# 16-head attentions: in odd steps a group of value matmuls stands in front of the scores instead of behind them

## The reference

```
def _L1_xattn_ref(q, k, v, Wq, bq, Wk, bk, Wv, bv, Wo, bo):
    B, L, D, H = (4, 512, 256, 16)
    ...
    qh = _split_heads(q @ Wq.T + bq)
    kh = _split_heads(k @ Wk.T + bk)
    vh = _split_heads(v @ Wv.T + bv)
    scores = jnp.einsum('bhqd,bhkd->bhqk', qh, kh) * SCALE
    attn = jax.nn.softmax(scores, axis=-1)
    out = jnp.einsum('bhqk,bhkd->bhqd', attn, vh)
    out = out.transpose(0, 2, 1, 3).reshape(q.shape[0], q.shape[1], D)
    return out @ Wo.T + bo
...
x = x + _L1_xattn_ref(_layernorm(x, axis=-1), ctx_1024, ctx_1024, ...)
...
x = x + _L3_xattn_ref(_layernorm(x, axis=-1), ctx_1024, ctx_1024, ...)
```

## Time and profile before

| what | value |
|---|---|
| median of 3 runs | 1415.19 us (1411.68 to 1415.5) |
| profiled execution | 1412.58 us, span 1410.6 us |
| TensorE busy | 1255.1 us, 89% of the span |
| VectorE, ScalarE, GpSimd busy | 60%, 33%, 33% |
| mean granted clock of TensorE | 0.962 of full speed |
| first attention, steps 0 to 63 | from 337.00 to 546.99 us of the span |
| second attention, steps 0 to 63 | from 976.98 to 1185.37 us |

### The profile page before, as it was taken

The page is one execution under the profiler, slowest core; times in us unless marked ns, Lnnn a source line. Parts: engine busy times, 40 slices in busy tenths (PEclk is TensorE's granted clock), DMA queues, the critical chain, the costliest instruction groups (busy, mean ns, idle before and its releaser), DMA issues. The chain is left out here.

```text
span 1410.6 us, 31497 instructions
## 1 busy us (share of the span) xinstructions
PE 1255.1 (89%) x9884; PEld 1003.2 (71%) x9884; DVE 851.2 (60%) x2809; ACT 472.5 (33%) x1119; POOL 472.2 (33%) x452
## 2 busy tenths in 40 slices
PE   4999789997899998799898899898899998799995
PEld 3777589995566665598787666776566665599994
DVE  6788444445677776344575477664566776366663
ACT  3556111112556554011111244443555554011110
POOL 1244612223224434422322256532134343222231
PEclk9999899998999999899999999999999999899998
DMA  9001334322101301564554100000001111645523
GB/s 309 36 24 40 113 112 137 126 65 75 46 24 39 133 33 54 198 196 140 169 180 144 47 14 1 1 1 23 8 24 40 33 44 46 226 94 138 138 48 86
DMA packets 86180, 120.07 MB, mean 85 GB/s; under 512 B 11248, under 2 KB 63600, under 8 KB 85776
## 3 DMA queue, kind: packets, MB, share of 16 engines
q1 hardware_dynamic: 45984, 51.53, 12.0%
q10 hardware_dynamic: 25856, 35.14, 7.8%
q0 software_dynamic: 14224, 31.92, 7.8%
HBM read 82.53 MB, written 38.13 MB: 86 GB/s over the span
## 5 line engine op out<-in xcount | busy, mean ns | idle before, releaser
L1342 PEld LDWEIGHTS bank<-f_xT,f_up 128*128 128x128 f32 x2144 | 263.2, 197 | 8.8 <-DVE f_xT L1216 3.7
L1342 PE MATMUL bank<-f_xT,f_up 128*128 128x128 f32 x2144 | 264.6, 280 | 2.1 <-DVE f_xT L1216 2.1
L415 DVE TENSOR_REDUCE mha_nmax<-bank 128x2 f32<-128x512 f32 x256 | 170.1, 686 | 112.4 <-PE bank L559 85.6
L1351 PE MATMUL bank<-f_down,f_hT 128*128 128x256 f32 x832 | 199.3, 382 | 1.7 <-DVE f_z L1289 1.4
L308 ACT ACTIVATE l_took<-bank 128x512 f32<-128x512 f32 x256 | 138.9, 598 | 143.6 <-PE bank L567 143.6
L559 PE MATMUL bank<-l_took,mha_q 32*128 32x256 f32 x1024 | 150.0, 411 | 40.6 <-DVE mha_nmax L415 28.9
L1351 PEld LDWEIGHTS bank<-f_down,f_hT 128*128 128x128 f32 x832 | 150.6, 191 | 21.0 <-DVE f_z L1289 2.3
L1109 POOL DMA_INDIRECT yout<-f_y,f_to x66 | 81.3, 1232 | 245.3 <-DVE f_y L1293 108.1
L559 PEld LDWEIGHTS bank<-l_took,mha_q 32*128 32x128 f32 x1024 | 91.4, 190 | 81.0 <-DVE mha_nmax L415 54.5
L567 PE MATMUL bank<-l_took 32*128 32x256 f32 x1024 | 145.5, 406 | 0.7 <-ACT l_took L308 0.7
L1156 ACT ACTIVATE f_hT<-bank,f_b 128x128 f32<-128x128 f32 x148 | 46.2, 363 | 280.9 <-PE bank L1342 280.9
(11 more groups left out here) (294 smaller groups left out, 2268.0 us busy)
## 6 DMA issues: line engine op xcount, KB each, us to landing
f_up<-in_W ACTq DMA_DIRECT2D x26, 512.0 KB, 4.8
l_took<-rows SPq DMA_DIRECT2D x91, 132.0 KB
f_down<-in_W ACTq DMA_DIRECT2D x20, 512.0 KB, 5.7
l_took<-rows SPq DMA_DIRECT2D x21, 264.0 KB, 2.7
ring<-yout SPq DMA_DIRECT2D x8, 512.0 KB, 4.1
mha_ctxT<-in_ctxT SPq DMA_DIRECT2D x16, 256.0 KB, 2.8
f_up<-in_W SPq DMA_DIRECT2D x6, 512.0 KB, 5.7
f_up<-in_V ACTq DMA_DIRECT2D x6, 512.0 KB, 4.4
```

The lines of the kernel that those rows point to most:

```text
L415: vector.tensor_reduce(nmax[:, p, :, at], ps_s[n % 2][:, :].rearrange("p (k s) -> p k s", s=S), AX.X, ALU.min).then_inc(max_ready, 1)
L1342: ins = pe.matmul(into, up[q][i][:, c, m * P:(m + 1) * P], xT[:, c, :], start=c == 0, stop=c == DC - 1)
L1351: ins = pe.matmul(ps_y[:, 0:D], hT[:, m, :], down[q][:, m, :], start=m == 0, stop=m == HC - 1)
```

## The change

In the loop over the steps of TensorE's program, the value group of an odd step moves from behind scores(u) to a place in front of it. Nothing is added or removed, and no other engine's program changes.

```
@@ -654,11 +654,11 @@
         for u in range(LAST):
             b, s = divmod(u, PAIRS)
+            if u % 2 and u >= 5:
+                values((u - 5) // 2)
             scores(u)
             if u % 2 == 0 and u >= 2:
                 turn_maxima((u - 2) // 2)
-            if u % 2 and u >= 5:
-                values((u - 5) // 2)
             if s == 0 and b + 1 < B:
                 turn_x(b + 1)
```

## The result

The changed kernel takes 1425.4 us (median of 5 runs, 1423.52 to 1433.22), the kernel before 1415.19 (5 runs, 1411.68 to 1415.55). The ratio is 1.0095, with a 95% interval of 1.0063 to 1.0128: the change makes the kernel slower by about 0.95%, some 13.4 us. Ratios here are taken over all runs and are not the quotient of two medians, which would be 1.0072. That is the side that was forecast, and the time lies in the range. The profiled execution of after is the slowest of its five, 1433.22 us with a span of 1431.3; it is 20.64 us above that of before, twice the difference of the medians, so what it holds beyond the attentions has to be set apart first.

A forecast was written before the change was run, and what follows sets the result against it. TensorE, busy 1255.1 of 1410.6 us, was taken as the bound. 1412.58 + 10.5 for waits + 2.4 for the clock gave 1425.5 for the profiled execution, 1428.1 on the median; predicted 1427, range 1419 to 1434.

The forecast's parts named there:

- The release of the values: Even steps: moved values wait for exponentials until 2.37 us after the previous S; bounds 0.05 or some 0.1 after their end.
- The rival that the values are not held: Even steps: the group starts before 1.84 us after S and fits under 2.84; 1413.8 us, no change; chance 0.07.
- VectorE's 2.51: Odd steps: VectorE's two maxima and the release hold S to S at 2.51 us or more, even without the group.
- the new wait: Step 6 of a middle batch: turn_maxima waits for the first half of encode on VectorE, 0.35 us more.
- The rival without this wait: turn_maxima finds encode done; a middle batch costs +0.04 us, the sum without clock falls is 1419.6; chance 0.08.
- the wait of the last batch: Even steps of the last batch: L594 on TensorE waits for ScalarE's exponentials (L308), some 1.0 us.
- step 4 to 8: First batch of each attention: 1.00 us added ahead of step 5 and 0.53 between steps 6 and 7, +1.53.
- batch 1: No routing in step 6, so step 6 to 7 ends with VectorE; 26.38 us against 26.32, +0.06.
- batches 2 to 6: Middle batches: 26.88 us against 26.49, +0.39 each, 5 x 0.39 = 1.95 per attention.
- last batch: Three even steps go from 2.84 to 3.37 us, three odd ones are 2.51; 23.97 against 22.26, +1.71 per attention.
- clock: First attention: falls to the lower clock at the first batch's end (0.88 us) and last batch (1.53), 2.4 together.
- The rival of more falls: Each of the four batch ends (two first, two last) loses two more clock falls at about 1.2 us; 1432.7; chance 0.13.

The follow-up runs named there:

- The kernel with the older group: Against the change: value groups in front but one pair of steps later, ScalarE's output copy ahead of its exponentials; 1408.9 us, ratio 0.9973 to before.
- the change's repeat: The change run again without an edit, beside two kernels with parts of it on one chip; 1429.06 us, ratio 1.0119 to before.
- the change with the lesser filling: The change plus unread matmuls in each attention's first batch, 4 behind step 3, 2 each behind steps 5, 6, 7; 1425.48 us, ratio 1.0093 to before.
- the kernel before with fillings: The kernel before plus unread matmuls in the first batches, 4 behind step 3 and 3 behind step 6; 1410.82 us, ratio 0.9988.

## Why the prediction was right, and which term was off

**The release of the values** was right: 2.36 to 2.39 after S, for 2.37. Of its two bounds the lower one held, 0.06 behind the exponentials. The kernel with the older group shows the cause by its absence, as far as the moved copy allows. The rival that the values are not held falls with it, and so does the other way of reading it, that the place in front costs by itself.

**VectorE's 2.51** held for steps 5 to 6 (2.51), and for the odd steps of the last batch (537.83 - 535.33 = 2.50). In step 3 to 4 it was 2.57, which VectorE's timeline of after explains:

```profile
435.81 1.29 DVE L415 TENSOR_REDUCE mha_nmax<-bank 128x2 f32<-128x512 f32 x2 [1.82 <-issue]
...
444.78 0.42 DVE L433 TENSOR_TENSOR mha_enc<-bank,mha_rsum 128x256 f32<-128x256 f32 x1
```

The maxima start 1.22 after the S at 434.59 instead of 1.16. The second row is the new wait: the first encode ends at 445.20, turn_maxima starts at 445.35 with 0.37 of waiting (forecast 0.35). The rival without this wait falls. Two signs came out a little smaller than named: the wait of the last batch is 0.87 for some 1.0, and that batch takes 23.89 for 24 or more. One sign of being wrong did appear: the profiled executions differ by 7.2 us outside of the two attentions. Traces of kernels that change nothing there differ as much, so it doesn't refute the account, but it isn't explained either.

The sum, term by term, from the traces (us, after less before):

| part | forecast per attention | first | second |
|---|---|---|---|
| steps 0 to 4 of the first batch, not changed | 0 | -2.48 | +1.65 |
| step 4 to 8 | +1.53 | +3.29 | +2.12 |
| batch 1 | +0.06 | +1.45 | +1.07 |
| batches 2 to 6 | +1.95 | +2.38 | +2.29 |
| last batch | +1.71 | +1.63 | +0.10 |
| clock | 2.4 in the first | (in the rows above) | |
| sum | 12.9 for both | 6.27 | 7.23 |

The middle batches were forecast 0.12 too short each (26.88 for 27.00: 0.06 in step 3 to 4, 0.05 in step 6 to 7), some 0.4 an attention. **The term that was mis-sized is the clock**, less in its size than in its place. The forecast put falls at the first batch's end (+0.88) and the last batch (+1.53) of the first attention. In this execution both last batches ran at 1.00, the second even gave back the fall that before had there (23.79 at 0.93), which is why it grew by only 0.10. The falls came at the first batch's end, 10.52 at 0.71 for 8.70 at full speed, and in batch 1 behind it, 27.77 and 27.43 where it takes 26.34 at full speed. In other executions of the study last batches were hit as well (0.86 and 0.93 above). That 12.9 comes so near to the 13.5 measured is partly luck: the first attention was forecast at +7.65 and grew by 6.27, with -2.48 in steps that no moved group touches, and the second at +5.25 and grew by 7.23.

How much the clock costs in the median can be read from the executions themselves, since the mean granted clock of each is recorded. Over the 23 runs of before beside the change's repeat, a clock lower by 0.001 goes with 0.75 us more (correlation -0.74), over six of the change with 0.94. (Three other sets of runs of before give 0.50, 0.55 and 0.93, so this is a loose measure.) The change ran at 0.9615 on average, before at 0.9661: 4.6 thousandths, 3.5 to 4.3 us, against 2.4 forecast. Of the 1.19%, some 16.8 us, that leaves about 13 for the waits. With the first batch filled the change ran at 0.9635 beside 0.9645, by the same slopes about 1 us of its 0.93% (13 us), which leaves 12. The sum has 10.5 for the waits, 11.3 with the 0.4 an attention that the middle batches were short. This is an estimate from what goes together.

The traces hold a more direct comparison. The second attention of the change with the lesser filling (first row), and that of the kernel before with fillings (second row), had no half-speed stretch at all:

```profile
983.68:1193.75 210.07, 190.10 (x1988) 127.38 (x1988) 136.99 (x380) 111.58 (x234) 65.28 (x62) 1.00 0.09 30
...
978.81:1183.20 204.39, 187.49 (x1983) 126.52 (x1982) 137.08 (x380) 111.31 (x233) 65.24 (x62) 1.00 0.09 30
```

They differ by 5.68 us where the sum has 5.25: 1.6 in steps 4 to 8, 0.0 in batch 1, 2.4 in batches 2 to 6 and 1.7 in the last batch, for 1.53, 0.06, 1.95 and 1.71. So the waits cost 11.4 us in two attentions without any help of the clock, for 10.5 forecast. Of the whole, 13.4 us in the first measurement and 16.8 in the repeat, 2.0 to 5.4 are left for the clock and all else, for 2.4 forecast. It is one execution of each; a kernel in which every fall is kept away was not run, so the share of the clock stays open within some us.

**The rival of more falls** (1432.7, 20 us above before) was wrong as a time, though the repeat's 16.8 us lie between it and the 12.9 of the forecast, and half right as a mechanism. The Trainium skill (TensorE: Matmul & The Clock Gate, "A second HAM failure mode: psum-queue depth-cycling") says of one kernel that frequent short idle times between its groups of matmuls made the clock swing and that the price was paid at the swings, between the bursts. The trace agrees as far as falls behind waiting stretches go (0.71 in 358.74:369.26). It doesn't where the pattern lasts longest: both last batches of after, with TensorE busy for 17.59 of 23.89 us, were granted 1.00 throughout. That is one execution: in others the last seven steps of the same order had 0.93 (the repeat) and 0.86, in part of the stretch and never in all of it.

## What to carry to other kernels

Work that is moved in front of a wait fills it only if its own inputs are there before that wait ends: compare the release of the moved instruction (2.37 here) with the end of the wait (2.84), less its own length (1.00). What the old place gives back ends at the next loop (2.51), so move only the groups whose old gap stays above that loop without them (4.00 less 1.00, but not 3.10 less 1.00, which had no wait either). The 24 of 60 moves chosen so made the kernel 0.64% faster where all of them made it 0.95% slower. Keep the price of each gap in a list: it forecasts the part as well as the whole.

## What was unexpected of the hardware

A batch in its old order took longer (27.16 for 26.32), at a granted clock of 0.94, behind a batch whose order had changed. The same last seven steps took 23.71 and 21.42 in one execution, at 0.86 and 1.00. And the fillers that kept the first batch at 1.00 did not shorten the kernel measurably: alone they gave a ratio of 0.9988 [0.997, 1.0005], although the way from step 4 to step 5 of the first batch fell from 4.81 and 4.78 to 3.18 and 3.17.
